# Three transfers for the keys' rows, and a bank of its own for each half's sums

## The chip, the cores and the metric

The kernel runs on one core of a Trainium2 chip. The metric is the device time of one execution in microseconds (us), the median of several runs. TensorE (PE) multiplies matrices into PSUM, which has eight banks of 128 partitions by 512 f32 (here `PS[:, 0..7, :]`); VectorE (DVE) and ScalarE (ACT) read the banks; GpSimd (POOL) works beside them; SyncE (SP) issues the DMA transfers between the memory in SBUF and the DRAM.

## The reference

Eight sublayers on a residual stream x of 2 batches by 1024 tokens by 128 channels, each fed a layer norm and added to x: a grouped-query attention with rotary position and low-rank updates (L0_attn_a), an expert layer (L0_ffn), a cosine attention of 16 heads (L0_attn_b), L0_ffn again, an attention of 16 heads of 8 channels (L1_attn_a), L1_ffn, an RWKV scan, and L1_ffn again. The change concerns the attentions of L1_attn_a and of the two L1_ffn. Both have 16 heads of width 8:

```python
# L1_attn_a: at this kernel's sizes and shapes every query block of 128 sees
# the keys that the mask `triu(ones(ws, end), k=1)` leaves of it
scores = einsum('bhqd,bhkd->bhqk', wq, wk) * scale
attn = softmax(where(mask, neg, scores)); out = einsum('bhqk,bhkd->bhqd', attn, wv)
# L1_ffn: x + attention(layernorm(x)) and then the experts; attention is causal
att = einsum('bhqd,bhkd->bhqk', q, k) / sqrt(hd)
att = where(tril(ones((t, t))), att, -inf); att = softmax(att)
y = einsum('bhqk,bhkd->bhqd', att, v)
```

In L1_attn_a the mask of a block of 128 queries has its diagonal at key 0, so row r of each block sees keys 0 to r: 128 keys are all that any query ever sees. In L1_ffn 1024 keys are seen causally.

## The kernel before, in words

All the attentions of 16 narrow heads go through `four_heads` (L519), four heads of one batch at a time: 8 groups (`ng`). A group is cut into units (`units_of`, L455): one half of the queries (a side of 512, so side 0 and side 1) against one block of 128 keys. With 128 keys (`nk` is 1, L1_attn_a) a group has `nu` = 2 units, one for each side. With 1024 keys (both L1_ffn) it has 12. The flag `use_max` is set in these three stages and not in L0_attn_b, which has another ring and other loads.

For each unit TensorE computes the scores with keys on partitions (`cols`, L665, with the mask added by L669), in two visits of two heads; ACT takes the exponential of each visit's two banks out of PSUM into `probs` (L799); and two units later (`LAG` = 2) TensorE multiplies the probabilities with the values (`values`, L685), which adds up one side of a group in bank 7: `start=kt == 0` opens it, and it is read when the side is complete. ACT copies it to `o_sum` (`evict`, L770), TensorE turns it (the "divide" job, L744), and DVE divides it by the sums (L896, L899). Since both sides add up in the one bank 7, the first product of a side waits until the side before is copied out:

```python
if kt == 0 and U:
    pe.wait_ge(evicted, 2 * g + side)
```

The exponential needs the maximum of each row first. So each group has side jobs that run a while ahead, `lead` groups before its own units (2 with 128 keys, 1 with 1024). A "rows" job computes scores with queries on partitions (`scores`, L697, mask L701) into a spare bank, and DVE reduces them to a negative maximum (L878). When the last of a group's are in, DVE splits the maxima in three bf16 parts (L840 to L842), TensorE turns them (the "turn" job, L739), DVE copies them to SBUF (L887) and SP stores them as rows 72 to 74 of the stacked queries (`load_c`, L613 or L615). TensorE's `cols` of that group waits for that transfer. The jobs are written out in one order (`side_jobs`, L477), which TensorE and DVE follow alike: four "rows" jobs in each unit with 128 keys, two after `cols`' first visit and two after its second, then the turn, then the divide. They take the spare banks in turn: `ring` = (4, 5, 6), and job n waits until DVE has read job n - 3 (`n - len(ring) + 1` reads). On ACT the order is: first visit's exponential, the copy of a finished side, second visit's exponential.

The matmuls' operands are the stacks `k_stack` (`S.Kst`) and `q_stack` (`S.Qst`): 72 rows for the 3 by 3 products of bf16 parts of 8 channels, so the 24 rows of the keys' parts stand three times under each other, and each of the queries' 24 rows three times in sequence. Both are read from DRAM by `load_group` with a broadcast (L605, L606), one transfer each, from `k_parts` and `q_parts`. For 1024 keys such a transfer moves 576 KB; for 128 keys the keys' moves 72 KB and the queries' 576 KB. There are room for `SLOTS` groups (4 or 3) in the stacks. SP issues everything from one queue in this order: group 0, the rows of ones (L627), further groups, the turned maxima, the store of batch 1's parts (L622), and then per group `load_group` and `load_c`. With 128 keys a group's load stands before the turned maxima of another group (`lead == 2`), with 1024 keys behind them. TensorE's first job of a group waits for its loads: `pe.wait_ge(loaded[g % SLOTS], per_group * (g // SLOTS + 1))`.

Of the kernel before, what the change touches and what calls it, by code (L numbers as in the profile page):

```python
# [19 lines left out]
ACT = mybir.ActivationFunctionType  # L20
# [4 lines left out]
NT = T // P  # L25
TT = B * NT
N = B * T
HALF = 512
# [408 lines left out]
def short_keys(S, b, keys):  # L437
    return S.k_parts[b, :, :, 0:NH * keys].rearrange("d j (h t) -> d j h t", t=keys)


def homes(S, b, n, i, keys, use_max):


    if n == 0:
        return [S.q_parts[b, i]]
    if use_max:
        return [short_keys(S, b, keys)[:, i]]
    return [S.k_eight[b, c] for c in ((0, 1, 2), (3, 4, 5), (6, 7))[i]]
# [6 lines left out]
def units_of(nk):  # L455

    out = []
    for side in range(2):
        js = range(4 * side, 4 * side + 4)
        for kt in range(nk(js[-1])):  # L460
            out.append((side, kt, P * next(n for n, j in enumerate(js) if nk(j) > kt)))
    return out
# [52 lines left out]
def last_unit(units, side):  # L515
    return max(u for u, x in enumerate(units) if x[0] == side)


def four_heads(S, Q, K, V, AO, nk, tri, use_max, SLOTS):  # L519
# [6 lines left out]
    units, PS, nu, ng = units_of(nk), S.PS, len(units_of(nk)), B * NH // 4  # L526
# [5 lines left out]
    turn_at = {e: k for k, e in enumerate(turns)}  # L532
    first, second = row_jobs(nk)
    last_rows = {e: number["rows", e[1], (second if second and e[2][-1] else first)[-1]] for e in turns}
    pairs, ring = (2, (4, 5, 6)) if use_max else (3, (6,))
    rows_of_stack, per_group, per_batch = (75, 32, 96) if use_max else (64, 128, 176)
    keys = P * nk(NT - 1)
    total = ng * nu
    second_batch = {(0, 1, 2)[i] if nu < 4 else (1, 4, 7)[i]: i for i in range(3)}
# [3 lines left out]
    def masked_units(U):  # L543

        return sum(meets(units[V % nu]) for V in range(U + 1))

    def meets(unit):
        side, kt, _ = unit
        return tri == "window" or 4 * side <= kt < 4 * side + 4
# [18 lines left out]
    with phase(S, 25) as (block, sems):  # L568
        (cols_ready, exp_done, masked, pv_done, evicted, job_ready, job_read, split_done, c_split, c_copied,
         summed, part_done, rest_done, zeroed, v_ready, ones_set, stored) = sems[:17]  # L570
        loaded, c_loaded = sems[17:21], sems[21:25]
# [7 lines left out]
        def slot(g, i):  # L579
            return 4 * (g % SLOTS) + i if use_max else 2 * (g % SLOTS) + i // 2  # L580

        def stack(i):

            return slice(0, rows_of_stack) if use_max else slice(64 * (i % 2), 64 * (i % 2) + rows_of_stack)

        @block.sync
        def _(sp):
            def load_group(g):
                b, h0 = divmod(4 * g, NH)
                if g >= SLOTS:  # L590
                    sp.wait_ge(cols_ready, visits[nu * (g - SLOTS + 1)])
                if b:
                    sp.wait_ge(stored, per_batch)
                at = slice(slot(g, 0), slot(g, 3) + 1)
                for i in range(0 if use_max else 2):
                    heads = slice(h0 + i, h0 + i + 3, 2)
                    sp.dma_start(S.Kst[stack(i), at, :],
                                 S.k_eight[b, :, :, heads, 0:keys].rearrange("c d h t -> (c d) h t")).then_inc(loaded[g % SLOTS], 16)
                    for r0, parts in ((0, 3), (24, 3), (48, 2)):
                        sp.dma_start(S.Qst[64 * i + r0:64 * i + r0 + HD8 * parts, at, :],  # L600
                                     S.q_parts[b, 0:parts, :, heads, :].rearrange("j d h t -> (j d) h t")).then_inc(loaded[g % SLOTS], 16)
                if use_max:
                    k_rows = short_keys(S, b, keys)[:, :, h0:h0 + 4, :].rearrange("d j h t -> (d j) h t")
                    q_rows = S.q_parts[b, :, :, h0:h0 + 4, :].rearrange("j d h t -> (j d) h t")
                    sp.dma_start(S.Kst[0:72, at, :], k_rows.unsqueeze(0).to_broadcast([3, 24, 4, keys])).then_inc(loaded[g % SLOTS], 16)  # L605
                    sp.dma_start(S.Qst[0:72, at, :], q_rows.unsqueeze(1).to_broadcast([24, 3, 4, T])).then_inc(loaded[g % SLOTS], 16)  # L606

            def load_c(e):
                k, g, sides = turn_at[e], e[1], e[2]
                sp.wait_ge(c_copied, k + 1)  # L610
                at, to = slice(slot(g, 0), slot(g, 3) + 1), slice(HALF * sides[0], HALF * (sides[-1] + 1))
                if len(sides) == 2:
                    sp.dma_start(S.Qst[72:75, at, to], S.ct[0:96, k % 2, :]).then_inc(c_loaded[g % SLOTS], 16)  # L613
                for i in range(4 if len(sides) == 1 else 0):
                    sp.dma_start(S.Qst[72:75, slot(g, i), to], S.ct[12 * i:12 * (i + 1), k % 2, :]).then_inc(c_loaded[g % SLOTS], 16)  # L615

            def store_batch():
                for i in range(3):
                    for n in range(2):
                        sp.wait_ge(part_done, 2 * i + n + 1)  # L620
                        for to in homes(S, 1, n, i, keys, use_max):
                            sp.dma_start(to.rearrange("d h t -> h d t"), S.parts[:, n, i, 0:part_width[n]]).then_inc(stored, 16)  # L622

            load_group(0)
            if use_max:
                for row in range(72, 75):
                    sp.dma_start(S.Kst[row:row + 1, :, :], S.ones_b[0:4 * SLOTS * keys // P, :]).then_inc(ones_set, 16)  # L627
            for g in range(1, SLOTS if lead == 2 else 1):
                load_group(g)
            for e in turns:  # L630
                if e[1] < lead:
                    load_c(e)
                    if e[2] == (0,):
                        load_group(lead)
            for g in range(SLOTS if lead == 2 else 1 + sum(e[2] == (0,) for e in turns), SLOTS):
                load_group(g)
            store_batch()
            for g in range(ng):
                if lead == 2 and g + SLOTS < ng:
                    load_group(g + SLOTS)  # L640
                for e in turns:
                    if e[1] == g + lead and g + lead >= lead:
                        load_c(e)
                if lead < 2 and g + SLOTS < ng:
                    load_group(g + SLOTS)

        @block.tensor
        def _(pe):
# [24 lines left out]
            def values(U):  # L673
                g, u = divmod(U, nu)
                side, kt, c0 = units[u]
                b, h0 = divmod(4 * g, NH)
                pe.wait_ge(exp_done, visits[U + 1])
                if u == 0 and h0 == 0:
                    pe.wait_ge(v_ready, b + 1)
                if not use_max and meets(units[u]):  # L680
                    pe.wait_ge(masked, masked_units(U))
                if kt == 0 and U:
                    pe.wait_ge(evicted, 2 * g + side)
                for i in range(4):
                    m = pe.matmul(PS[32 * i:32 * (i + 1), 7, c0:HALF], S.Vx[:, NT * b + kt, h0 + i, :],  # L685
                                  S.Pt[:, U % PBUFS, i, c0:HALF], start=kt == 0, stop=u == last_unit(units, side),
                                  skip_group_check=True)
                m.then_inc(pv_done, 1)
# [58 lines left out]
            for s, events in enumerate(steps):  # L747
                U = s - 1
                mid = sum(e[0] == "rows" for e in events) // 2 if U >= 0 else 0
                if 0 <= U < total:  # L750
                    cols(U, 0)
                for e in events[:mid]:
                    side_job(e)
                if 0 <= U - LAG < total and (U - LAG) % 2:
                    values(U - LAG - 1)
                    values(U - LAG)
                if 0 <= U < total and not narrow(U):
                    cols(U, 1)
                for e in events[mid:]:
                    side_job(e)  # L760

        def evict(eng, V):
            (g, u), side = divmod(V, nu), units[V % nu][0]
            if u == last_unit(units, side):
                out = 2 * g + side
                eng.wait_ge(pv_done, V + 1)
                if out >= 2:
                    eng.wait_ge(job_read, number["divide", (out - 2) // 2, out % 2] + 1)
                if use_max:
                    eng.activation(S.Oc[:, out % 2, :], PS[:, 7, :], ACT.Copy).then_inc(evicted, 1)  # L770
                else:
                    eng.tensor_copy(S.Oc[:, out % 2, :], PS[:, 7, :]).then_inc(evicted, 1)

        @block.scalar
        def _(act):
# [50 lines left out]
        def _(dve):  # L826
# [17 lines left out]
            for s, events in enumerate(steps):  # L844
                V = s - 1 - LAG
                if not use_max and 0 <= V < total:
                    evict(dve, V)
# [1194 lines left out]
```

## Time and profile before

| | |
|---|---|
| median of 3 runs | 2552.72 us (2546.31 to 2552.99) |
| profiled execution, its own time | 2555.11 us |
| its span | 2553.4 us |
| busy PE, DVE, ACT, POOL | 83%, 63%, 56%, 31% of the span |
| mean granted TensorE clock | 0.902 of full speed |

The span is what the profiler's records cover of the execution; the rest of its time lies around it. The stages follow each other with a barrier between them, so the shares of the whole say little of a single one: each of the three stages that the change touches is read in its own window. L1_attn_a's attention with 128 keys ("the window stage" below, after the name that its jobs have) begins at about 1425 us; the two causal stages of L1_ffn ("the causal stages") begin at about 1564.5 and 2104.9 us.

### The profile page before, as it was taken

To read this page: it belongs to the slowest core of one execution; us is meant where nothing else is said; L and a number is where in the kernel's file an instruction comes from. 1 tells how busy PE (TensorE), PEld (TensorE's weight loads), DVE (VectorE), ACT (ScalarE), POOL (GpSimd) and SP (SyncE) were. 2 spreads that over 40 slices of the span, in tenths; PEclk is the share of its full clock that TensorE was granted. 3 is DMA by queue.
4 is the path that set the end of the run, shared out by engine and by line. 5 is a ranking of instruction groups with operands and counts; after the bars stand their busy time and mean duration, and the time that the engine had idled before them with its cause. 6 is when DMAs were issued, how large, how long until landed. Compare 5 with 4: busy or idle time off the path is not lost. (4 is left out here: it accounts for less than half of the span.)

```text
span 2553.4 us, 36997 instructions
## 1 busy us (share of the span) xinstructions
PE 2120.8 (83%) x13716; PEld 1249.8 (49%) x13716; DVE 1609.2 (63%) x3495; ACT 1422.9 (56%) x2088; POOL 781.1 (31%) x426
## 2 busy tenths in 40 slices
PE   4999999999999826578618785999989747999798
PEld 2666666666666423522314443444447523444367
DVE  5888788787886556631365645777523686777324
ACT  3777777777777461379551342566643252666541
POOL 3877787777877201142101203100000022000000
PEclk8999999999999957789858897899989875999999
DMA  2000000000000050152130301211010002110100
GB/s 73 1 5 1 3 5 1 3 5 1 1 3 1 1 169 1 46 129 50 44 126 1 92 24 45 81 40 39 2 33 1 1 25 69 51 39 20 34 1 18
DMA packets 43117, 82.11 MB, mean 32 GB/s; under 512 B 8170, under 2 KB 17018, under 8 KB 39930
## 3 DMA queue, kind: packets, MB, share of 16 engines
q1 hardware_dynamic: 42938, 79.73, 11.0%
q8 instruction: 111, 1.82, 0.3%
q14 instruction: 68, 0.56, 0.1%
HBM read 64.09 MB, written 14.88 MB: 31 GB/s over the span
## 5 line engine op out<-in xcount | busy, mean ns | idle before, releaser
L799 ACT ACTIVATE probs<-psum_banks 128x1024 f32<-128x1024 f32 (+3 forms) x544 | 442.7, 864 | 309.5 <-PE psum_banks L669 247.9
L878 DVE TENSOR_REDUCE neg_max<-psum_banks 128x1 f32<-128x512 f32 (+3 forms) x672 | 406.3, 658 | 174.2 <-PE psum_banks L701 112.3
L1230 POOL TENSOR_SCALAR l0a_rows<-l0a_rows,l0a_rinv 128x1024 f32<-128x1024 f32 x160 | 454.6, 2846 | 187.9 <-DVE l0a_rinv L1192 184.1
L1180 DVE TENSOR_REDUCE l0a_nmax<-psum_banks 128x1 f32<-128x1024 f32 x256 | 312.5, 1221 | 139.8 <-PE psum_banks L1074 137.9
L665 PE MATMUL psum_banks<-q_stack,k_stack 75*128 75x512 bf16 (+7 forms) x1216 | 283.1, 337 | 54.1 <-ACT probs L799 26.4
L1126 ACT ACTIVATE l0a_rows<-psum_banks,l0a_nmax 128x1024 f32<-128x1024 f32 x256 | 286.0, 1117 | 60.4 <-DVE l0a_nmax L1180 59.1
L697 PE MATMUL psum_banks<-k_stack,q_stack 72*128 72x128 bf16 (+3 forms) x1024 | 249.5, 325 | 59.0 <-DMA q_stack<-q_parts 53.4
L1088 PE MATMUL psum_banks<-packed,l0a_rows 128*128 128x128 f32 x2048 | 267.1, 273 | 2.0 <-POOL l0a_rows L1230 0.9
L1073 PE MATMUL psum_banks<-l0a_kh,l0a_qw 128*128 128x512 f32 x512 | 242.6, 474 | 21.5 <-POOL l0a_qw L1219 13.8
L1088 PEld LDWEIGHTS psum_banks<-packed,l0a_rows 128*128 128x128 f32 x2048 | 239.1, 141 | 42.4 <-issue 4.8
L685 PE MATMUL psum_banks<-probs,v_ones 128*32 128x512 f32 (+3 forms) x2432 | 239.9, 505 | 9.9 <-ACT o_sum L770 6.5
L1074 PE MATMUL psum_banks<-l0a_kl,l0a_qw 128*128 128x512 f32 x512 | 205.3, 401 | 0.0
L665 PEld LDWEIGHTS psum_banks<-q_stack,k_stack 75*128 75x128 bf16 (+1 forms) x1216 | 89.0, 97 | 221.4 <-ACT probs L799 106.4
L433 POOL TENSOR_SCALAR l1f_y<-x_res,ln_mv,ln_rstd 128x128 f32<-128x128 f32 x32 | 26.0, 825 | 545.6 <-DVE ln_rstd L404 545.6
L1073 PEld LDWEIGHTS psum_banks<-l0a_kh,l0a_qw 128*128 128x128 f32 x512 | 97.9, 191 | 144.0 <-ACT l0a_rows L1126 77.0
L697 PEld LDWEIGHTS psum_banks<-k_stack,q_stack 72*128 72x128 bf16 x1024 | 93.4, 103 | 152.9 <-DMA q_stack<-q_parts 51.3
L1796 DVE SCALAR_TENSOR_TENSOR l1f_y<-psum_banks,rt_g,l1f_y 128x128 f32<-128x128 f32 x256 | 72.1, 344 | 103.6 <-PE psum_banks L1734 103.6
L1758 ACT ACTIVATE l1f_h<-psum_banks 128x512 f32<-128x512 f32 x128 | 75.7, 599 | 106.6 <-PE psum_banks L1720 106.3
L1147 DVE SCALAR_TENSOR_TENSOR l0a_ts<-psum_banks,l0a_sin 32x512 f32<-32x512 f32 x192 | 131.9, 687 | 4.2
L1121 ACT ACTIVATE x_norm<-psum_banks 128x512 f32<-128x512 f32 x128 | 76.2, 595 | 97.9 <-PE psum_banks L1088 97.7
L669 PE MATMUL psum_banks<-tri_k,ident_b 128*128 128x128 bf16 (+1 forms) x576 | 129.6, 242 | 0.0
L1100 PE MATMUL psum_banks<-x_norm,l0a_v 128*64 128x512 f32 x512 | 124.0, 604 | 6.0 <-ACT l0a_ot L1131 6.0
(285 smaller groups left out, 3419.5 us busy)
## 6 DMA issues: line engine op xcount, KB each, us to landing
q_stack<-q_parts SPq DMA_DIRECT2D x24, 576.0 KB
k_stack<-k_parts SPq DMA_DIRECT2D x16, 576.0 KB
qkv<-in_l0f_w SPq DMA_DIRECT2D x6, 1024.0 KB, 5.5
moe_b<-in_l0f_b SPq DMA_DIRECT2D x32, 128.0 KB, 3.7
k_stack<-k_eight SPq DMA_DIRECT2D x16, 256.0 KB
l1f_w<-in_l1f_w SPq DMA_DIRECT2D x16, 256.0 KB, 4.7
q_stack<-q_parts SPq DMA_DIRECT2D x32, 96.0 KB
q_parts<-parts SPq DMA_DIRECT2D x12, 256.0 KB
```

What stands on the lines that cost most here:

```text
L665: m = pe.matmul(PS[:, bank, to], S.Kst[stack(i), slot(g, i), kt * P:(kt + 1) * P], S.Qst[stack(i), slot(g, i), side * HALF + c0:(side + 1) ...
L685: m = pe.matmul(PS[32 * i:32 * (i + 1), 7, c0:HALF], S.Vx[:, NT * b + kt, h0 + i, :], S.Pt[:, U % PBUFS, i, c0:HALF], start=kt == 0, stop= ...
L697: return pe.matmul(bank[:, at:at + k1 - k0], S.Qst[0:72, slot(g, i), jq * P:(jq + 1) * P], S.Kst[0:72, slot(g, i), k0:k1], start=first, st ...
L799: act.activation(S.Pt[:, U % PBUFS, 2 * half:2 * half + 2, c0:HALF], PS[:, bank:bank + 2, c0:HALF], ACT.Exp).then_inc(exp_done, 1)
L878: dve.tensor_reduce(out, scores, AX, ALU.max, negate=True).then_inc(job_read, 1)
L1073: pe.matmul(scores(s)[:, c0:c0 + HALF], q, R.Kh[:, b, c0:c0 + HALF], start=True, stop=False)
L1074: m = pe.matmul(scores(s)[:, c0:c0 + HALF], q, R.Kl[:, b, c0:c0 + HALF], start=False, stop=True)
L1088: m = pe.transpose(PS[:, 4 + a, jj * P:(jj + 1) * P], R.Pr[:, (NT * ps + 2 * jj + a) % RING, kt * P:(kt + 1) * P], S.ident[:])
L1126: act.activation(R.Pr[:, s % RING, :], scores(s), ACT.Exp, bias=R.nmax4[:, s % 4:s % 4 + 1], accum_out=R.rsum4[:, s % 4:s % 4 + 1]).then_i ...
L1147: ins = dve.scalar_tensor_tensor(R.t_sin[to, u % 3, :], PS[src, bank_of(job), :], scale_of(job), R.sinT[src, job[2] % 2 * HALF:(job[2] % 2 ...
L1180: dve.tensor_reduce(R.nmax4[:, s % 4:s % 4 + 1], scores(s), AX, ALU.max, negate=True).then_inc(max_done, 1)
L1230: rows_divided.mark(pool.tensor_scalar(R.Pr[:, s % RING, :], R.Pr[:, s % RING, :], R.rinv4[:, s % 4:s % 4 + 1], None, ALU.mult))
```

## The change

The keys' rows are loaded by three transfers of 24 rows each, in the place of one with a broadcast, in all three stages with `use_max`; the wait on the group's loads goes to 64 accordingly. With 128 keys (`nu < 4`), side 0 adds up in bank 6 and side 1 in bank 7, and a side waits for the copy of the side two before instead of one before; the side jobs then have banks 4 and 5 alone. With 1024 keys banks and waits stay as they were.

```diff
-    pairs, ring = (2, (4, 5, 6)) if use_max else (3, (6,))
-    rows_of_stack, per_group, per_batch = (75, 32, 96) if use_max else (64, 128, 176)
+    pairs, ring, sums = (3, (6,), (7, 7)) if not use_max else (2, (4, 5), (6, 7)) if nu < 4 else (2, (4, 5, 6), (7, 7))
+    sums_apart = sums[0] != sums[1]
+    rows_of_stack, per_group, per_batch = (75, 64, 96) if use_max else (64, 128, 176)
...
                     k_rows = short_keys(S, b, keys)[:, :, h0:h0 + 4, :].rearrange("d j h t -> (d j) h t")
                     q_rows = S.q_parts[b, :, :, h0:h0 + 4, :].rearrange("j d h t -> (j d) h t")
-                    sp.dma_start(S.Kst[0:72, at, :], k_rows.unsqueeze(0).to_broadcast([3, 24, 4, keys])).then_inc(loaded[g % SLOTS], 16)
+                    for copy in range(3):
+                        sp.dma_start(S.Kst[24 * copy:24 * (copy + 1), at, :], k_rows).then_inc(loaded[g % SLOTS], 16)
                     sp.dma_start(S.Qst[0:72, at, :], q_rows.unsqueeze(1).to_broadcast([24, 3, 4, T])).then_inc(loaded[g % SLOTS], 16)
...
-                if kt == 0 and U:
-                    pe.wait_ge(evicted, 2 * g + side)
+                if kt == 0 and U > sums_apart:
+                    pe.wait_ge(evicted, 2 * g + side - sums_apart)
                 for i in range(4):
-                    m = pe.matmul(PS[32 * i:32 * (i + 1), 7, c0:HALF], S.Vx[:, NT * b + kt, h0 + i, :],
+                    m = pe.matmul(PS[32 * i:32 * (i + 1), sums[side], c0:HALF], S.Vx[:, NT * b + kt, h0 + i, :],
...
                 if use_max:
-                    eng.activation(S.Oc[:, out % 2, :], PS[:, 7, :], ACT.Copy).then_inc(evicted, 1)
+                    eng.activation(S.Oc[:, out % 2, :], PS[:, sums[side], :], ACT.Copy).then_inc(evicted, 1)
```

## Rows read from the trace of the kernel before

**Rows 1.** Busy time by stretch: start:end, length, engines, clock, DMA share, GB/s.
```profile
1425.30:1532.00 106.70, 86.81 (x648) 44.77 (x648) 56.77 (x143) 44.10 (x55) 14.31 (x8) 0.94 0.24 61
1564.50:1862.50 298.00, 267.48 (x2041) 123.73 (x2041) 199.47 (x398) 162.87 (x215) 17.74 (x8) 0.91 0.14 39
```
**Rows 2.** Who waited for whom, PE, causal stages: total, times, longest, us.
```profile
PE psum_banks L697 <- DMA q_stack<-q_parts: 21.6, 2, 20.1
...
PE psum_banks L697 <- DMA q_stack<-q_parts: 21.0, 2, 19.8
```
**Rows 3.** Timeline, first causal stage: start, length, engine, line, instruction [idle before <-releaser].
```profile
1564.54 0.75 SPq L605 DMA_DIRECT2D k_stack<-k_parts  x1
1565.34 0.85 SPq L606 DMA_DIRECT2D q_stack<-q_parts  x1
1579.46 0.61 PE L697 MATMUL psum_banks<-k_stack,q_stack 72*128 72x128 bf16 x4 [20.11 <-DMA q_stack<-q_parts]
...
1594.99 0.72 SPq L605 DMA_DIRECT2D k_stack<-k_parts  x1
1609.14 0.59 PE L697 MATMUL psum_banks<-k_stack,q_stack 72*128 72x128 bf16 x4 [1.46 <-DMA q_stack<-q_parts]
```
**Rows 4.** Busy time by stretch, the same stage's load and its clock.
```profile
1567.00:1568.00 1.00, 0.00 (x0) 0.00 (x0) 0.00 (x0) 0.00 (x0) 1.00 (x1) 0.50 0.75 145
1571.00:1572.00 1.00, 0.00 (x0) 0.00 (x0) 0.00 (x0) 0.00 (x0) 0.94 (x3) 0.50 0.49 84
1573.00:1574.00 1.00, 0.00 (x0) 0.00 (x0) 0.00 (x0) 0.00 (x0) 0.94 (x1) 0.50 0.20 82
1600.00:1608.00 8.00, 7.68 (x28) 3.17 (x26) 6.86 (x12) 4.71 (x6) 4.20 (x2) 0.50 0.29 89
1616.00:1624.00 8.00, 7.46 (x42) 2.29 (x34) 5.06 (x11) 4.30 (x6) 3.42 (x2) 0.84 0.43 95
```
**Rows 5.** Timeline, start of the window stage.
```profile
1426.26 0.84 SPq L606 DMA_DIRECT2D q_stack<-q_parts  x1
1432.09 0.61 PE L697 MATMUL psum_banks<-k_stack,q_stack 72*128 72x128 bf16 x4 [10.82 <-DMA q_stack<-q_parts]
```
**Rows 6.** Timeline, window stage: one round of its steady part.
```profile
1472.33 1.06 PE L685 MATMUL psum_banks<-probs,v_ones 128*32 128x512 f32 x8
1473.46 0.60 ACT L770 ACTIVATE o_sum<-psum_banks 128x512 f32<-128x512 f32 x1 [5.34 <-PE psum_banks L685]
1473.95 1.94 ACT L799 ACTIVATE probs<-psum_banks 128x1024 f32<-128x1024 f32 x2
1474.20 1.06 PE L685 MATMUL psum_banks<-probs,v_ones 128*32 128x512 f32 x8 [0.81 <-ACT o_sum L770]
1475.20 0.10 PEld L665 LDWEIGHTS psum_banks<-q_stack,k_stack 75*128 75x128 bf16 x1 [0.84 <-ACT probs L799]
1476.73 1.29 DVE L878 TENSOR_REDUCE neg_max<-psum_banks 128x4 f32<-128x512 f32 x2 [3.44 <-PE psum_banks L701]
1476.97 0.60 PE L744 MATMUL psum_banks<-packed,o_sum 128*128 128x128 f32 x4
1478.73 0.39 PE L697 MATMUL psum_banks<-k_stack,q_stack 72*128 72x128 bf16 x4
1479.31 0.29 DVE L899 TENSOR_TENSOR qkv<-psum_banks,sum_inv 128x128 f32<-128x128 f32 x1
1480.93 0.22 PE L739 MATMUL psum_banks<-ident_b,c_split 128*96 128x128 bf16 x1
1481.45 0.66 PE L744 MATMUL psum_banks<-packed,o_sum 128*128 128x128 f32 x4 [0.30 <-DVE neg_max L878]
1483.80 0.64 PE L685 MATMUL psum_banks<-probs,v_ones 128*32 128x512 f32 x4
```
**Rows 7.** Timeline, window stage: group 4's load and the late turned maxima.
```profile
1458.12 0.85 SPq L606 DMA_DIRECT2D q_stack<-q_parts  x1
1459.02 0.77 SPq L613 DMA_DIRECT2D q_stack<-c_turned  x1
1465.96 0.38 PE L665 MATMUL psum_banks<-q_stack,k_stack 75*128 75x512 bf16 x1 [1.89 <-issue]
```

More of the change, by code:

```diff
@@ L769, in evict @@
                 if use_max:
-                    eng.activation(S.Oc[:, out % 2, :], PS[:, 7, :], ACT.Copy).then_inc(evicted, 1)
+                    eng.activation(S.Oc[:, out % 2, :], PS[:, sums[side], :], ACT.Copy).then_inc(evicted, 1)
                 else:
-                    eng.tensor_copy(S.Oc[:, out % 2, :], PS[:, 7, :]).then_inc(evicted, 1)
+                    eng.tensor_copy(S.Oc[:, out % 2, :], PS[:, sums[side], :]).then_inc(evicted, 1)
         @block.scalar
```

## The prediction

> **What bounds the kernel now.** I cut the span into the three stages that the change touches, since a barrier closes each. TensorE is busy 86.8 of 106.7 us in the window stage and 267.5 of 298.0 us in the first causal one [rows 1]; it is the engine to follow in all three. So I read what TensorE waited for. In each causal stage its largest wait is on a load: 21.6 us in two waits, and 21.0 us in the second stage [rows 2]. The timeline shows the two: 20.11 us before the stage's first matmul at 1579.46 us, and 1.46 us before 1609.14 us, when group 1's load is late [rows 3]. What holds the load is seen in the stretches of 1 us: until 1572 us the DMA engines are half to three quarters busy at 84 to 145 GB/s (and up to 217 between), and in every stretch from 1573 until the first matmul only a share of 0.20 is busy at 82 GB/s [rows 4]. 0.20 of 16 engines is 3: the keys' transfer, whose outermost dimension is the broadcast of 3, runs on three engines, and 7 us long it runs alone, the queries' having ended. No other instruction is needed before the first matmul.
>
> The window stage's keys are an eighth as large, so it has no such tail; TensorE starts 5.83 us after the queries' issue began (1426.26 to 1432.09) [rows 5]. In its steady part a round of one group lasts 11.47 us (from the products at 1472.33 us to the next at 1483.80), and TensorE is idle only about 1.1 us of it: 0.81 between the two sides' products, for ACT's copy of the side before, and 0.30 before a divide, for a spare bank [rows 6].
>
> **The keys' transfers in the causal stages.** The keys' issue takes 0.75 us [rows 3], so two more put the queries' issue 1.5 to 1.6 us later, to 1566.9 us. Each new transfer has 24 rows outermost, as the queries' source has, so I expect it on as many engines: a share of 0.75, or 12. Lower bound of the landing: as in the window stage, 5.83 us after the queries' issue, the keys being done by then: 1572.7 us, 6.8 us earlier. Upper bound: 576 KB of keys and as much of queries (1.18 MB) at the mean of the five stretches from 1567 to 1572 us (148 GB/s; first and last are in [rows 4], 217, 156 and 139 between) take 8.0 us from 1567, with 0.6 us to the first matmul 1575.6 us, 3.8 us earlier. Keys' packets that run while the queries' are not yet issued should come near the lower one; I take 5.3 us earlier. Everything in the stage follows the first load, and ACT and POOL have their own work done by 1574 us, so the 5.3 us are whole on the path.
>
> Group 1's load (issue at 1594.99 us) lands 14.1 us later now [rows 3]; some 4 to 5 us less take it off the path, and the 1.46 us before 1609.14 us go. DVE is busy 6.86 of 8 us beside it [rows 4], so a part may come back as a wait on it: I count 1.2 us, from 0.8 to 1.5. Later loads are issued a full round ahead and nobody waits for them; the two added issues (1.5 us of SP) come behind the turned maxima there. Together 6.5 us in each causal stage, 13.0 us in both, with 9 and 16.5 as ends.
>
> The Trainium skill ("DMA: Bandwidth & Descriptors", Rules for kernel authors) says not to split a load into transfers to disjoint partitions, as they share the same engines and serialize. Here the share of 0.20 shows the one transfer on 3 engines of 16, so the split brings engines in rather than only dividing work. By that rule alone the 13.0 us would be nothing; that is the slower rival below. The same page (Why a DMA increments its semaphore by 16 and not by 1) has the number of engines set by the largest number up to 16 that divides the outermost sizes of both sides, 3 before and 12 after; the 3 agrees with the share.
>
> **The window stage's start.** Here the keys are small, and the two more issues ahead of the queries only delay them: +1.5 us at the first matmul. For the same reason every later load takes 1.5 us more of SP.
>
> **A bank for each side.** The wait of 0.81 us between the sides' products goes: the second begins at 1473.39 instead of 1474.20 us and ends near 1474.4. But the next matmul is `cols`' second visit, which waits for ACT's exponential of two visits before. ACT copies side 0 first (it starts at 1473.46, after side 0's product), and only then has that exponential, from 1473.95 us on; two take 1.94, so the first ends at about 1474.95, and the matrix load of L665 at 1475.20 us names it as its releaser [rows 6]. TensorE's own path arrives at the same 1475.20 us. So the wait moves behind the second product and is worth under 0.1 us a round. Only after the last group, where no `cols` follows, are the 0.8 us real: -0.8 us. Bounds: -0.8, and -6.5 if all eight such waits counted.
>
> **Two spare banks in place of three.** Job n now waits for DVE's reading of job n - 2. TensorE's start after a read is 0.06 us behind it. One round, from [rows 6]:
> - The divide at 1476.97 us shares a bank with the first of the two row jobs just before, which DVE reads until 1477.38: +0.47 us.
> - The second row job after it (1478.73) waits for the divide's reading, which ends at 1479.60 behind the five small operations that split the maxima: at 1479.66, and with the first stall it would have come at 1479.20: +0.46.
> - The turn (1480.93, now 1481.86) waits for the third of four reductions. They begin at about 1479.6 and later follow TensorE; the third ends near 1482.3: +0.5.
> - The divide behind it waits for the fourth, near 1482.95: +0.42, and the old 0.30 goes, so +0.12.
>
> A full round costs 1.55 us. The stage has no full round until the first divides: two turns alone at 0.5 each and one divide at 0.47 come first, 1.45 us. Behind the stall told next stand 0.62 (turn and divide) four times, 0.93 three times, and a last divide at 0.47: 5.7 us. Bounds: if DVE's reads come earlier than this by a tenth or two at each of the stalls, 3.5; with the wait for ACT pushed as well, 7.5.
>
> **The turned maxima behind group 4's load.** TensorE waits 1.89 us until 1465.96 for the turned maxima that SP issued at 1459.02, right behind group 4's queries [rows 7]. SP's side moves by 1.5 (start), 0.5 (the first turn) and 1.5 (two issues) = 3.5 us. TensorE's side moves by 1.5 + 1.45 = 2.95, so SP decides, and all up to here costs 3.5 us (2 to 4.5). The stage: 3.5 + 5.7 - 0.8 = +8.4 us, from 5 to 11.
>
> **Sum.** On the profiled execution: 2555.1 - 13.0 + 8.4 = 2550.5 us. The median of the runs lies 2.4 us under that execution (2552.7), so I forecast 2548.1 us.
>
> **Rivals.**
> - The clock rises earlier in the causal stages (faster). It is at 0.50, which is 1.2 GHz, until some 40 us after the first matmul, and rises within 1616 to 1624 us [rows 4]; between, TensorE pauses for the loads and for DVE. With one pause gone and the other shorter it may rise at the first products. From 1596 to 1618 us TensorE's work is the bound and would take half; DVE, busy 6.86 of 8, holds back most: 4 us a stage, 8 in both, 2540 us. Against it: it stayed low through 1600 to 1608 us with TensorE busy 7.68 of 8.
> - Separate sums pay (faster): all eight copies' waits go, 6.5 us, as ACT's exponentials come forward, and the two spare banks cost 3.5 us instead of 5.7. 2548.1 - 5.7 - 2.2 = 2540 us. Against it stands L665's wait for ACT.
> - The split brings nothing (slower): the three transfers and the queries' queue on the same engines, each at the slow pace of about 80 GB/s or held by the shared source rows, so that the first matmul stays near 1579.5 us. Then only the window stage's 8.4 us remain: 2561 us. It decides once the causal loads land less than 1 us earlier than before. Against it speaks the queries' transfer, with 24 outermost, above 140 GB/s.
>
> **How the numbers follow.** Within 0.3% (7.7 us, about what a measurement of this kernel can tell from no change) means 2545.1 to 2560.4. Forecast 0.57 (its own range 2543 to 2554); the early clock 0.15; separate sums 0.12; no gain of the split 0.07; the rest lies in the sizes: both causal terms at their upper end with the window stage at its lower give 2552.7 - 16.5 + 5 = 2541 (0.07), the reverse 2552.7 - 9 + 11 = 2555 (0.02). Faster 0.15 + 0.12 + 0.07 = 0.34, slower 0.08, within 0.58. The range takes in the two faster rivals and the reverse: 2537 to 2557 us.
>
> **What would show it.** Right: in the causal stages no stretch at a share of 0.20, the first matmul near 1574.2 us and no wait before group 1's; in the window stage L685 without its 0.81, and L665 waiting for ACT instead; L744, L697 and L739 waiting for L878 and L899 in every round, a round of 13.0 us, and the first matmul 1.5 us later. Wrong: rounds that stay at 11.5 us, a causal first matmul after 1576 us, or a full clock before 1605 us.

## The result

The changed kernel took 2542.73 us (median of 8 executions, 2539.14 to 2548.66) against 2552.85 us before (8 executions, 2546.31 to 2556.29): ratio 0.9963, 95% interval 0.9952 to 0.9974, about 9.4 us faster by the ratio and 10.1 by the medians. The forecast was 2548.1 us in a range of 2537 to 2557. The same kernel was run twice more, beside other experiments: ratios 0.9979 (0.9967 to 0.9990) and 0.9986 (0.9974 to 0.9999). Over all three, its 32 executions average 2546.2 us, against 2552.0 us for 77 of the kernel before: 5.8 us faster. Both kernels scatter over 13 to 15 us, which is why one comparison of 8 says less than its interval seems to. Two executions of later runs, 7130.42 us (the split in the window stage alone) and 9510.63 us (TensorE kept busy in its wait), stand far outside all others and are in no average or ratio here.

The profile after is of the execution with 2548.66 us (span 2546.9 us). Its stages begin at 1425.82, 1572.72 and 2104.60 us.

The timeline of the two causal stages' starts and of group 1 in the first (start, length, engine, line, instruction) answers to [rows 3]:

```profile
1572.72 1.37 SPq L607 DMA_DIRECT2D k_stack<-k_parts  x3
1574.15 0.89 SPq L608 DMA_DIRECT2D q_stack<-q_parts  x1
1583.36 0.61 PE L699 MATMUL psum_banks<-k_stack,q_stack 72*128 72x128 bf16 x4 [15.84 <-DMA q_stack<-q_parts]
1598.87 1.25 SPq L607 DMA_DIRECT2D k_stack<-k_parts  x3
1611.37 0.64 PE L699 MATMUL psum_banks<-k_stack,q_stack 72*128 72x128 bf16 x4
...
2104.60 1.15 SPq L607 DMA_DIRECT2D k_stack<-k_parts  x3
2114.42 0.60 PE L699 MATMUL psum_banks<-k_stack,q_stack 72*128 72x128 bf16 x4 [15.04 <-DMA q_stack<-q_parts]
```

From the stage's first issue to its first matmul it is 10.64 and 9.82 us; before it was 14.92 in the first stage [rows 3] and 14.64 in the second (2104.88 to 2119.52). Group 1's first row job, at 1611.37 us, has no wait before it. The stretches of 1 us of the same load answer to [rows 4] (the last two numbers are the DMA share and GB/s):

```profile
1573.00:1574.00 1.00, 0.00 (x0) 0.00 (x0) 0.00 (x0) 1.00 (x1) 1.00 (x1) 0.50 0.33 66
1574.00:1575.00 1.00, 0.00 (x0) 0.00 (x0) 0.00 (x0) 0.01 (x1) 1.00 (x1) 0.50 0.76 229
1577.00:1578.00 1.00, 0.00 (x0) 0.00 (x0) 0.00 (x0) 0.00 (x0) 1.00 (x1) 0.50 0.76 154
1579.00:1580.00 1.00, 0.00 (x0) 0.00 (x0) 0.00 (x0) 0.00 (x0) 0.94 (x2) 0.50 0.77 188
1581.00:1582.00 1.00, 0.00 (x0) 0.00 (x0) 0.00 (x0) 0.00 (x0) 1.00 (x2) 0.50 0.23 40
1582.00:1583.00 1.00, 0.00 (x0) 0.00 (x0) 0.00 (x0) 0.00 (x0) 0.11 (x1) 0.50 0.03 3
```

From 1574 to 1580 us the share is 0.74 to 0.86 (0.75 would be 12 of 16 engines); then come 0.60 and a single microsecond at 0.23. The six microseconds of before at 0.16 to 0.20 and 54 to 82 GB/s are gone. In TensorE's waits of the first causal stage, [rows 2] have become one wait on a load in place of two:

```profile
PE psum_banks L699 <- DMA q_stack<-q_parts: 15.8, 1, 15.8
```

In the window stage a round of the steady part now looks like this; the first and last line are SP's issues of the turned maxima of two successive groups. It answers to [rows 6].

```profile
1475.04 0.75 SPq L615 DMA_DIRECT2D q_stack<-c_turned  x1
...
1482.26 0.66 PE L746 MATMUL psum_banks<-packed,o_sum 128*128 128x128 f32 x4 [0.34 <-DVE neg_max L880]
1484.45 0.40 PE L699 MATMUL psum_banks<-k_stack,q_stack 72*128 72x128 bf16 x4 [0.21 <-DVE qkv L901]
1487.16 0.26 PE L741 MATMUL psum_banks<-ident_b,c_split 128*96 128x128 bf16 x1 [0.34 <-DVE neg_max L880]
1487.76 0.66 PE L746 MATMUL psum_banks<-packed,o_sum 128*128 128x128 f32 x4 [0.34 <-DVE neg_max L880]
1490.11 1.92 PE L687 MATMUL psum_banks<-probs,v_ones 128*32 128x512 f32 x16
1492.81 0.83 PE L667 MATMUL psum_banks<-q_stack,k_stack 75*128 75x512 bf16 x2 [0.78 <-ACT probs L801]
...
1487.86 0.74 SPq L615 DMA_DIRECT2D q_stack<-c_turned  x1
```

The 16 value products run without a break, L667 waits 0.78 us for ACT's exponential behind them, and the divide, the row job after it, the turn and the next divide each wait for DVE. A round takes 12.82 us (1475.04 to 1487.86) instead of 11.47. From SP's first load to its first store of the next stage the window stage takes 135.0 us instead of 127.2: +7.8. That is clear of the scatter of the stage: in the eight profiles of kernels that run it with three spare banks it takes 124.9 to 128.0 us, in the five with two (and ACT's order as it is) 134.3 to 135.0. From the first load of a causal stage to SP's next loads behind it (the experts' weights, `l1f_w`), the two take 292.7 and 291.0 us instead of 298.0 and 297.2: -5.3 and -6.2.

The window stage's first groups, before any steady round, changed too. The first block is of the kernel before, the others are of the changed one; in the stretches the third number from the end is the granted clock:

```profile
1433.00:1437.00 4.00, 4.00 (x26) 2.79 (x25) 3.19 (x5) 0.00 (x0) 4.00 (x4) 0.50 0.71 180
1437.00:1441.00 4.00, 2.99 (x26) 1.71 (x24) 3.67 (x11) 0.00 (x0) 0.23 (x1) 0.93 0.77 161
```
```profile
1437.00:1441.00 4.00, 4.00 (x25) 2.02 (x23) 3.13 (x5) 0.00 (x0) 0.68 (x2) 0.50 0.80 199
1445.00:1449.00 4.00, 4.00 (x25) 2.26 (x24) 2.55 (x4) 0.00 (x0) 0.00 (x0) 0.50 0.03 6
1449.00:1453.00 4.00, 3.78 (x19) 1.90 (x18) 2.94 (x9) 1.02 (x1) 0.00 (x0) 0.68 0.00 0
```
```profile
1442.96 0.61 PE L699 MATMUL psum_banks<-k_stack,q_stack 72*128 72x128 bf16 x4 [0.66 <-DVE neg_max L880]
1444.78 0.61 PE L699 MATMUL psum_banks<-k_stack,q_stack 72*128 72x128 bf16 x4 [0.68 <-DVE neg_max L880]
```

Before, the clock is at half until about 12 us after the stage's beginning and full from then on; after, it stays at half until about 25 us, and TensorE waits twice for DVE between its first row jobs. All 14 profiles of the case agree: full from 11 to 13 us on with three spare banks, from 22 to 26 us on with two. Why it rises later isn't settled: in the stretch ahead of its rise TensorE was busy 4.00 of 4 us in the kernel before, and it was as busy in two of the changed kernel's stretches at half clock.

### The profile page after: what moved, and what is told of

Its sections match the earlier page's. It is cut to its first block and busy times, and to the rows that moved or that the text cites. A ratio compares the mean times of both kernels' runs of the same rounds, so it can differ in the third digit from the quotient of the medians.

```text
span 2546.9 us, 37034 instructions
## 1 busy us (share of the span) xinstructions
PE 2124.5 (83%) x13706; PEld 1250.8 (49%) x13716; DVE 1610.5 (63%) x3495; ACT 1422.2 (56%) x2088; POOL 780.6 (31%) x426
## 5 line engine op out<-in xcount | busy, mean ns | idle before, releaser
L667 PE MATMUL psum_banks<-q_stack,k_stack 75*128 75x512 bf16 (+7 forms) x1216 | 284.0, 338 | 57.3 <-ACT probs L801 31.8
L687 PE MATMUL psum_banks<-probs,v_ones 128*32 128x512 f32 (+3 forms) x2432 | 238.3, 505 | 3.2 <-POOL probs L824 2.7
L667 PEld LDWEIGHTS psum_banks<-q_stack,k_stack 75*128 75x128 bf16 (+1 forms) x1216 | 89.3, 98 | 223.9 <-ACT probs L801 112.4
## 6 DMA issues: line engine op xcount, KB each, us to landing
moe_b<-in_l0f_b SPq DMA_DIRECT2D x32, 128.0 KB, 3.7
```

The source lines that it names most:

```text
L667: m = pe.matmul(PS[:, bank, to], S.Kst[stack(i), slot(g, i), kt * P:(kt + 1) * P], S.Qst[stack(i), slot(g, i), side * HALF + c0:(side + 1) ...
L687: m = pe.matmul(PS[32 * i:32 * (i + 1), sums[side], c0:HALF], S.Vx[:, NT * b + kt, h0 + i, :], S.Pt[:, U % PBUFS, i, c0:HALF], start=kt == ...
```

## The experiments

Each job timed four kernels and the kernel before on one chip. "Split" means the three transfers of the keys' rows.

**The split in the causal stages alone** (twice, in two jobs)

```diff
+                    if nu >= 4:
+                        for copy in range(3):
+                            sp.dma_start(S.Kst[24 * copy:24 * (copy + 1), at, :], k_rows).then_inc(loaded[g % SLOTS], 16)
+                    else:   # as before
```

> The three transfers only in the two causal stages; the window stage as in the kernel before. Theory (the causal loads give all of the gain and the window stage's banks take some back): first matmul of both causal stages 9.8 to 10.7 us after the stage's first issue (before: 14.9 and 14.6), no wait before group 1; median 11 to 15 us under the kernel before, so about 2540 us, 2 to 7 us under the changed kernel. Rival (the banks cost nothing over the runs, or gain, and the profiled execution showed them at their worst): no faster than the changed kernel, 8 to 11 us under before.

> Three transfers in the causal stages only, once more, beside the changed kernel in one job. Theory (the window stage's banks cost 7.8 us): 11 to 12 us under before and 4 to 7 us under the changed kernel. Rival (they cost nothing over many runs): equal to it.

Measured: 2540.63 us, ratio 0.9957 (0.9940 to 0.9974); again 2537.29 us, 0.9942 (0.9927 to 0.9958), while the changed kernel in that second job came to 2548.97 us. The 11 executions of both average 2539.3 us, 12.8 under the 77 of before and 6.9 under the 32 of the changed kernel. The rival (the banks cost nothing) is out: the window stage's part of the change takes back about half of what the loads bring. In its profile the stages take 126.1 (window), 292.3 and 290.6 us.

**The banks alone, and two spare banks with one bank for the sums**

```diff
-    pairs, ring = (2, (4, 5, 6)) if use_max else (3, (6,))
# banks alone: the changed kernel's line, with the keys in one transfer
+    pairs, ring, sums = (3, (6,), (7, 7)) if not use_max else (2, (4, 5), (6, 7)) if nu < 4 else (2, (4, 5, 6), (7, 7))
# two spare banks, sums of both sides in bank 7
+    pairs, ring = (2, (4, 5) if nu < 4 else (4, 5, 6)) if use_max else (3, (6,))
```

> Banks 6 and 7 for the two sides and two spare banks in the window stage; keys' rows in one transfer everywhere, as before. Theory: rounds of 12.8 us in place of 11.5, and the time 5 to 8 us above before. Rival (separate sums pay): same or up to 5 us under before.

> Window stage with two spare banks but one bank for both sides' sums (bank 6 left empty); nothing else changed. Theory: it costs what two spare banks cost, 1.4 to 1.6 us a round, 6 to 9 us above before, and 1 to 2 us more than the kernel with two spare banks and separate sums, whose only gains are 0.17 us a round and 0.8 us at the end. Rival (separate sums are worth their 0.81 us wait each): 5 us or more above that kernel.

Measured: banks alone 2559.38 us, 1.0034 (1.0021 to 1.0047); two spare banks with one sum bank 2561.13 us, 1.0038 (1.0023 to 1.0053). Both are slower than before, and they differ by 1.8 us, which two intervals of this width don't separate; the rounds in their profiles do: 12.82 us with the banks alone (as in the changed kernel), 12.99 with one sum bank, which keeps the old wait behind the first product:

```profile
1474.18 0.77 SPq L613 DMA_DIRECT2D q_stack<-c_turned  x1
1487.17 0.76 SPq L613 DMA_DIRECT2D q_stack<-c_turned  x1
...
1489.41 1.07 PE L685 MATMUL psum_banks<-probs,v_ones 128*32 128x512 f32 x8
1491.29 1.07 PE L685 MATMUL psum_banks<-probs,v_ones 128*32 128x512 f32 x8 [0.81 <-ACT o_sum L770]
```

So two spare banks cost 1.52 us a round (12.99 - 11.47), and separate sums give back 0.17 (12.99 - 12.82), though they remove a wait of 0.81.

**The split in the window stage alone**

```diff
+                    if nu < 4:   # three transfers; one, as before, with 1024 keys
```

> Three transfers only in the window stage, banks as before. Theory: first matmul 0.5 to 1 us later, since the two more issues take 0.4 us each, and the turned maxima behind group 4's load as much later: 1 to 2 us above before, hard to tell from none. Rival: the smaller keys' rows land sooner on more engines and it comes out under before.

Measured: 2556.47 us, 1.0016 (1.0004 to 1.0028). The size, 4 us, is above what I expected and above what its profile shows: the window stage takes 127.1 us there, 127.2 before, and its first matmul comes 0.4 us later (7.10 us after the first issue, 6.72 before). The interval reaches down to 1 us. There is no gain; how much of the 4 us is a cost isn't settled.

**ACT's copy behind the second exponential**

```diff
-                    if use_max and half == 0 and 0 <= U - LAG < total:
+                    if use_max and half == (1 if nu < 4 and U < total else 0) and 0 <= U - LAG < total:
                         evict(act, U - LAG)
```

> The changed kernel with one edit: in the window stage ACT copies a finished side after the second visit's exponential, not before it. Theory (the separate sums bring nothing because the next matmul waits for an exponential that ACT puts behind the copy): TensorE's idle 0.78 us a round before L667 goes, 5 to 6 us under the changed kernel. Rival (something else holds that matmul, or the wait moves to the next exponential): within 1.5 us of the changed kernel.

Measured: 2544.00 us, against 2548.97 us for the changed kernel in the same job (0.9969, 0.9958 to 0.9980, against 0.9986). By averages of 12 executions the difference is 3.8 us, not the 5 to 6 expected, and the two intervals overlap; the profile is clearer. The window stage takes 131.4 us, against 134.3 to 135.0, and its round is 11.98 us, 0.84 shorter:

```profile
1475.14 0.75 SPq L615 DMA_DIRECT2D q_stack<-c_turned  x1
1487.12 0.74 SPq L615 DMA_DIRECT2D q_stack<-c_turned  x1
...
1489.37 1.92 PE L687 MATMUL psum_banks<-probs,v_ones 128*32 128x512 f32 x16
1490.50 0.60 ACT L772 ACTIVATE o_sum<-psum_banks 128x512 f32<-128x512 f32 x1 [4.25 <-PE psum_banks L687]
1491.22 0.39 PE L667 MATMUL psum_banks<-q_stack,k_stack 75*128 75x512 bf16 x1
```

L667 follows the products at once. That shows where the 0.81 us had gone: the exponential that L667 needs stood behind the copy in ACT's order. With that order separate sums give back 1.01 us a round (12.99 - 11.98), still less than the 1.52 that the third spare bank is worth, and the kernel stays behind the split alone in the same job (2544.00 against 2537.29 us).

**Six transfers in place of three**

```diff
+                        for copy in range(6):
+                            sp.dma_start(S.Kst[12 * copy:12 * (copy + 1), at, :], k_rows[copy % 2 * 12:copy % 2 * 12 + 12]).then_inc(loaded[g % SLOTS], 16)
```

> As the split in the causal stages alone, but six transfers of 12 rows. Theory (what counts is on how many DMA engines a transfer runs, 12 in both, not how many transfers there are): first causal matmul at most 1.5 us later than with three, for three more issues of 0.4 us; 9 to 12 us under before. Rival (it is the cut in pieces that speeds the load): first matmul 1 us or more earlier than with three transfers.

Measured: 2543.36 us, 0.9969 (0.9958 to 0.9980), with the split in the causal stages only. Its first causal matmul comes 11.38 us after the first issue, against 10.87 with three transfers (1566.37 to 1577.24 us); in the second stage it is 11.69 against 9.62, more than the 1.5 us that I allowed:

```profile
1566.03 3.07 SPq L607 DMA_DIRECT2D k_stack<-k_parts  x6
...
1577.41 0.61 PE L701 MATMUL psum_banks<-k_stack,q_stack 72*128 72x128 bf16 x4 [16.59 <-DMA q_stack<-q_parts]
```

More pieces don't speed the load, so cutting alone isn't the gain. What sets three transfers apart from one is the DMA share, 0.74 to 0.86 against 0.16 to 0.20 at the end of the load. That the number of engines is the cause is argued from it: one transfer of the keys on 12 engines, or three on 3 engines each, was not run.

**TensorE kept busy in the wait for the causal load**

```diff
+            for _ in range(WARM if use_max and nu >= 4 else 0):   # WARM = 32
+                pe.matmul(PS[:, 0, :], S.ident_b[:], S.tri_k[:], start=True, stop=True, skip_group_check=True)
```

> Three transfers in the causal stages only, and TensorE multiplies 32 times the identity by the 512 mask columns into bank 0 while it waits for the first load there (the results are overwritten). Theory (the clock stays at half speed for some 35 us behind the load because TensorE came out of an idle wait, and TensorE is the bound from the first exponentials on): full clock at the first matmul, and each causal stage 5 to 9 us shorter than with the split alone; about 2528 us. Rival (DVE's reductions bound that stretch and the clock falls again between its jobs): within 3 us of the split alone.

Measured: 2541.94 us, 0.9955 (0.9941 to 0.9969): no gain over the split alone. The stretches of its first causal stage show why (after the engines' busy times: granted clock, DMA share, GB/s):

```profile
1568.00:1576.00 8.00, 6.62 (x37) 3.01 (x35) 0.59 (x1) 0.00 (x0) 5.40 (x4) 0.96 0.45 88
1576.00:1584.00 8.00, 6.81 (x30) 1.85 (x28) 7.86 (x17) 0.00 (x0) 0.00 (x0) 0.89 0.00 0
1584.00:1592.00 8.00, 5.13 (x16) 1.55 (x16) 5.81 (x12) 0.20 (x1) 0.00 (x0) 0.50 0.17 43
1592.00:1600.00 8.00, 8.00 (x29) 3.35 (x28) 6.54 (x12) 5.06 (x6) 3.38 (x2) 0.50 0.46 110
1600.00:1608.00 8.00, 8.00 (x43) 5.22 (x42) 7.32 (x17) 1.55 (x4) 0.83 (x1) 0.50 0.00 0
```

The clock was full for most of the first row jobs (at 2.4 GHz in place of 1.2), but DVE was the busier engine there, 7.86 of 8 us; in the next stretch TensorE was busy 5.13 of 8 us, waited for the maxima, and the clock was at half again, where it stayed through two stretches in which TensorE was busy all the time. The first causal stage took 295.1 us (292.3 and 292.8 with the split alone), the second 290.5 (290.6 and 291.0).

**The turned maxima ahead of group 4's load**

```diff
-                if lead == 2 and g + SLOTS < ng:
+                if lead == 2 and 0 < g < ng - SLOTS:
                     load_group(g + SLOTS)
...
-                if lead < 2 and g + SLOTS < ng:
+                if (lead < 2 or g == 0) and g + SLOTS < ng:
```

> Three transfers in the causal stages only, and in the window stage group 2's turned maxima issued before group 4's load. Theory: the third group's wait of 1.2 to 1.9 us goes, 1 to 2 us under the split alone. Rival: no difference that can be measured.

Measured, with the causal split: 2539.72 us, 0.9953 (0.9936 to 0.9970), against 2537.29 us for the split alone in the same job. The wait for the maxima is gone, and a row job behind it waits for DVE's reading in its place:

```profile
1465.51 0.38 PE L701 MATMUL psum_banks<-k_stack,q_stack 72*128 72x128 bf16 x4 [1.17 <-DVE qkv L903]
```

Together with the busy wait (a run of both) it gave no more:

> As the split with the busy wait, and in the window stage group 2's turned maxima are issued before group 4's load. Theory: the 1.89 us wait of TensorE at its third group goes, 1 to 2 us under the split with the busy wait, unless group 4's queries then land too late for their row jobs. Rival: no difference.

Measured: 2542.54 us, 0.9964 (0.9952 to 0.9976).

**The changed kernel again** (twice)

> The changed kernel itself once more, in one job with the kernels that follow. The parts measured alone (split in the causal stages -11.2 us, banks +7.5) add up to -4, and the changed kernel was measured at -10.1. Theory (the parts add; the first measurement of the changed kernel fell low among executions that scatter over 10 us): 4 to 8 us under before. Rival (the banks cost less beside the earlier causal loads than alone): 9 to 11 us under before once more.

> The changed kernel once more, for the comparison in one job. Theory: 5 to 9 us under before. Rival: 10 us or more.

Measured: 2546.34 and 2548.97 us. The parts do add: causal split -12.8, banks +7.5 (alone), together -5.3, against -5.8 over 32 executions. The split in the window stage isn't in this sum; with the 4 us measured for it alone it would be -1.3, so the sum agrees with its profile (no cost) better than with its time. The first comparison's -10 was a favourable draw of 8.

## Why the prediction was right, step by step

The time was in the range, and the kernel became a little faster, by the two opposite terms of the sum. How near it came is in part luck. By the ratio of the first comparison, 0.9963, the time lies outside the 0.3% around before, a case to which I gave 0.34; the average of all 32 executions, 0.23% under before, lies within, to which I gave 0.58. And in the window stage two errors cancelled, as told below.

- *First causal load, 5.3 us (3.8 to 6.8).* The mechanism was as told: a share of 0.20 before, 0.76 after. The size was 4.3 us in the first stage and 4.8 in the second. The issues were cheaper than I took (three in 1.15 to 1.37 us, I had 2.25). But when the queries' issue ended, at 1575.04 us, only some 0.3 MB of the 1.18 had moved (the two stretches from 1573 us, at 66 and 229 GB/s), so the keys were not done by then, as my lower bound had it. The stretches from 1574 to 1581 us moved 135 to 229 GB/s, 167 in the mean, not far above the 148 of my upper bound, and the first matmul came near that bound.
- *Group 1's load, 1.2 us.* The wait went: group 1's first row job comes 38.65 us after the stage's first issue, 44.60 before, 1.7 us more than the first matmul gained, and part of that came back later. The stages came out 5.3 and 6.2 us shorter, 5.7 and 6.6 with the split alone (298.0 - 292.3 and 297.2 - 290.6), and 12.8 over its executions; the sum said 6.5 each and 13.0.
- *Window stage's start, +1.5 us.* It was 0.6: from first issue to first matmul 7.31 us (1425.82 to 1433.13) after and 6.72 (1425.37 to 1432.09) before. I had priced a plain issue like one with a broadcast, 0.75 us; it takes 0.4 (three in 1.16 us here).
- *Separate sums, under 0.1 us a round.* 0.17, by the mechanism named (L667 waits for ACT); the run with ACT's other order shows it.
- *Two spare banks, 1.55 us a round.* 1.52 with one sum bank, 1.35 with two. All four stalls stand at the four instructions foretold, at 0.21 to 0.34 us by their labels. The labels show less than the stalls cost: a matmul's record here lasts 0.38 us and the next one starts 0.22 us after it, and the label counts only the idle time after the record's end. From start to start the stalls of this round are 0.50, 0.37, 0.50 and, for the second divide, 0.08 us (0.60 against 0.52 before); I had 0.47, 0.46, 0.50 and 0.12.
- *Turned maxima behind group 4's load, +3.5 us up to there.* TensorE takes up group 2 at 44.5 us into the stage (1470.33 - 1425.82), 40.6 before (1465.96 - 1425.37): +3.9. The size is near by luck; both paths to it were mis-sized. SP issued the maxima 5.0 us later (38.67 us into the stage, 33.65 before), not 3.5: by the kernel's own wait, group 4's load starts when TensorE is through with the scores of group 0 (at 1462.42 us, 36.60 into the stage, 31.96 before), so SP's side moves with TensorE's, which I had counted apart. And TensorE was ready 5.3 us later (43.99 us into the stage against 38.70), not 2.95, so that 0.52 us is left of the old wait of 1.89. Its first matmul was only 0.6 us late, but at the first products (L687 at 1464.17 us, L685 at 1458.84) it was 4.9 us behind: with two spare banks the row jobs of the first group wait for DVE, and the clock stayed at half 10 to 14 us longer. The prediction had no term for either, and no run tells the two apart.
- *The stage, +8.4 us.* 7.8 in the profile, 7.5 for the banks alone: 3.9 up to group 2 and 3.9 behind it, where the sum had 3.5 and 4.9.
- *The rivals.* No gain of the split: out, by 12.8 us. Separate sums pay: out as the kernel stands. The clock: it didn't rise at the first products. In the changed kernel's profiles it was full from 46 to 50 us after a causal stage's beginning on, from 53 to 54 us before; from the first matmul that is 36 to 39 us, and 38 to 39 before, so it came earlier mainly by what the load did. Lifting it early brought nothing, because the stretch that it was to shorten was reached at half clock again. The rival looked at the causal stages alone; the larger change of the clock was in the window stage, where it rose later.

Best of all that ran is the split in the causal stages with the window stage as before: 2540.63 and 2537.29 us, faster than either kernel. What was added to it (2539.72 to 2543.36 us) gained nothing more.

## What to carry to other kernels

A DMA share that sits at a few sixteenths while the load is awaited can point to a transfer whose outermost dimension is small (here 0.20 with 3 outermost, about 0.75 with 24); write the copies of a broadcast as transfers of their own, and check that no compute waits on the longer issue list. Before removing a wait, look for what stands behind the same releaser in its engine's order: here the copy was waited for twice, once by the product and once, through ACT's order, by the next matmul. And a PSUM bank taken from a ring of three is paid at every point where a small batch of other work delays the reader, 1.52 us a round here, and again in the first groups of the stage.

## What was not expected of the hardware

- Issuing a transfer with a broadcast on its source took SP 0.69 to 0.85 us in the kernel before (0.72, 0.75 and 0.85 in [rows 3]), a plain one of 24 of its rows 0.37 to 0.46 us (three in 1.12 to 1.37).
- The scatter of 10 us and more between executions of one text lies partly in stretches that no edit touches. The last 151 or 147 us of three profiles, from the last causal stage's end, hold the same 736 matmuls; they differ by the granted clock (0.91 or 0.93):

```profile
2395.60:2546.90 151.30, 133.19 (x736) 97.24 (x736) 58.69 (x254) 48.79 (x81) 0.00 (x0) 0.91 0.08 22
```
```profile
2391.70:2539.10 147.40, 129.83 (x736) 95.14 (x736) 58.65 (x254) 48.79 (x81) 0.00 (x0) 0.93 0.07 22
```

The first is of the changed kernel, the second of the causal split alone; another profile of the changed kernel had 147.3 us and 0.93. Over all 14 profiles the stretch takes 147.4 us in five and 150.6 to 151.5 in nine, whichever the kernel. Such a draw of 4 us in one stretch is two thirds of the 5.8 us that the change moved over its 32 executions.
